# Fold in passes, one load on ScalarE's queue, x loads between the weights, a halved first q group, and three pieces of work at other places

## The chip, the cores and the metric

The kernel runs on one core of a Trainium2 chip. The metric is the device time of one execution in microseconds (us), the median of the runs. A core has five engines that run their own instruction lists side by side and wait for each other by semaphores: TensorE (PE, matmuls and transposes, results into the PSUM banks), VectorE (DVE), ScalarE (ACT), GpSimd (POOL) and SyncE (SP), which issues the loads and stores (DMAs).

## The reference

One Perceiver block in fp32 with T = 512 query rows of D = 512 and a context of 8192 rows:

```python
qp, kp, vp = LN(x) @ Wq.T + bq, ctx @ Wk.T + bk, ctx @ Wv.T + bv
x = x + softmax(qp @ kp.T / sqrt(32)) @ vp @ Wo.T + bo      # one head of width 512
q, k, v = split(LN(x) @ W_qkv); q, k = relu(rms(q)*qn), relu(rms(k)*kn)   # 16 heads of 32
x = x + (q @ (k.T @ v) / (q . sum(k) + 1e-6)) @ W_out + b_out             # linear attention
x = x + routed_experts(LN(x)) + causal_depthwise_conv(LN(x), 4 taps) + conv_b
```

The routed part has 4 gated MLPs of width 256 and 4 simple terms, and takes the best 2 of 8 for each row.

## The kernel before, in words

**Precision.** Each fp32 product is made of three fast matmuls: a matrix is split into a high part `_h` (rounded, type fp32r) and a low part `_l` (the rest), and `project` (L1400 on) sums high x high, high x low and low x high in PSUM. The high part is a copy by ScalarE (`high_...`) or GpSimd, the low part a subtraction by VectorE (`low_...`) or GpSimd (`split_wo`, `wq_l`).

**Opening.** PE multiplies `wv` by `wo` (512x512 each) in C = 4 blocks e over the contraction into four PSUM banks (`fold_part`, the fold). Block 0 has its own code (`first_part` for the first two column blocks, with 256-column halves of `wo`). A block is 12 full-width matmuls: for each c the three products one after the other. Meanwhile x (4 tiles t of 128 rows) is normalised: VectorE's `first_stats(t)`, ScalarE's `std_of(t)`, VectorE's `ln_scale(t)` (reciprocal and shift), ScalarE's `apply_of(t)`, which writes `xn`. PE transposes a tile (`transpose_x(t)`, 4 small instructions) at four places in blocks 2 and 3 of the fold; ScalarE (`high_xT`) and VectorE (`low_xT`) split it from PSUM into `xT`. Then come the q groups: for each e, 12 full-width matmuls of `wq` with all of `xT`. Each engine does its part in a hand-written order, and waits where an operand isn't there.

The loads of this stage are issued by SP one after the other: the halves of `wv` and `wo` block 0 (128 KB each), then `wv`, `wo` and x tiles (256 KB each), then `wq`, `wk` and the first context tiles.

**Attention.** The context comes in 64 tiles of 128 keys, two to a load. PE's `scores(s)` makes tile s (12 matmuls) in one of two banks, so tile s waits until VectorE's `peak(s - 2)` has taken the maximum from that bank (semaphore `max_done`), and every second tile for `low_ct`. ScalarE's `keep(s)` copies the scores to a ring first. The weighting of values follows 22 tiles later. VectorE's list in one step s is: subtractions and sums of older tiles, `low_ct` (s even), block maxima, `peak(s)`, and then odd jobs: at s = 1 `sum_key_terms()` (sums of `qb` over the four groups), at s = 3 `key_terms()` (a transpose and sums down to `key_bias`, first used at s = 17), at s = 9 `biases()`.

**Linear attention.** `linear(t)` multiplies tile t of q by the k-v product (8 PE instructions), VectorE divides by the normaliser into `heads[t]`, PE transposes (`transpose_heads(t)`), ScalarE and VectorE split, and PE projects with `wout` (12 matmuls a tile). PE's order was linear 0, 1, 2, 3, then heads 0, heads 1, then the projections.

Of the kernel before, what the change touches and what calls it, by code (L numbers as in the profile page):

```python
# [11 lines left out]
P = 128  # L12
D = 512
# [58 lines left out]
def perceiver_block(nc, x, ctx_t, ctx_n, wq_t, wk_in, wv_in, wo_t, wqkv_in, wout_in, pieces, cols_in, rows_in, out):  # L72
    with ExitStack() as stack:
# [318 lines left out]
        def _(sp):  # L392
            def load_wv(e):
                sp.dma_start(wv_raw[:, e, :], wv_in[e]).then_inc(wv_loaded[e], 16)
# [8 lines left out]
            def load_wo0(h):  # L403
                part = slice(h * HALF, (h + 1) * HALF)
                sp.dma_start(wo_raw[:, 0, part], wo_t[0][:, part]).then_inc(wo0_loaded[h], 16)

            def load_x(t):
                sp.dma_start(xs[:, t, :], x[t]).then_inc(x_loaded[t], 16)

            load_wv0(0)  # L410
            load_wo0(0)
# [5 lines left out]
            load_x(1)  # L417
            load_wo(2)
            load_wv(2)
            load_x(2)  # L420
            load_x(3)
            load_wo(3)
            load_wv(3)
            for e in range(C):
                sp.dma_start(wq_raw[:, e, :], wq_t[e]).then_inc(wq_loaded[e], 16)
# [210 lines left out]
        def _(act):  # L636
            def std_of(n):

                t = n % TT
                act.wait_ge(var_ready, n + 1)  # L640
                act.activation(std[:, t:t + 1], var[:, t:t + 1], ACT.Sqrt).then_inc(std_ready, 1)
# [23 lines left out]

            act.wait_ge(ones_ready, 1)
# [23 lines left out]
            apply_of(1)  # L690
            std_of(2)
            high_wv(3)
            high_xT(0, XT_BANKS)
            std_of(3)
            apply_of(2)
            apply_of(3)
            high_xT(1, XT_BANKS)
            high_xT(2, XT_BANKS)
            high_xT(3, XT_BANKS)
            high_wq(1)  # L700
# [184 lines left out]
        def _(dve):  # L885
# [58 lines left out]
            first_stats(0)  # L944
            first_stats(1)
            ln_scale(0)
            low_wv(2)
            ln_scale(1)
            first_stats(2)
            first_stats(3)  # L950
            low_wv(3)
            ln_scale(2)
            ln_scale(3)
            low_xT(0, XT_BANKS)
# [172 lines left out]
            for s in range(TILES + AHEAD - LEAD + 1):  # L1127
# [22 lines left out]
                if s == 1:  # L1150
                    sum_key_terms()
                if s == 3:
                    key_terms()
# [237 lines left out]
        def _(pe):  # L1391
# [34 lines left out]
            def fold_part(e, c):  # L1426

                ins = project(WVO_BANKS[c], [cut(wv, e, c * P, (c + 1) * P)], [cut(wo, e, 0, D)], starts=(e == 0),
                              stops=(e == C - 1))
                if e == C - 1:  # L1430
                    ins.then_inc(wvo_psum, 1)

# [19 lines left out]
            for c in range(2, C):  # L1452
                fold_part(0, c)

            transposed_at = {(2, 1): 0, (2, 3): 1, (3, 1): 2, (3, 3): 3}
            for e in range(1, C):
                pe.wait_ge(wv_ready, e)
                if e == 1:
                    pe.wait_ge(wo1_ready, 1)
                else:  # L1460
                    pe.wait_ge(wo_ready, e - 1)
                for c in range(C):
                    fold_part(e, c)
                    if (e, c) in transposed_at:
                        if transposed_at[e, c] == 0:
                            pe.wait_ge(ident_ready, 2)
                        transpose_x(transposed_at[e, c])

            pe.wait_ge(xl_ready, TT)
            for e in range(C):  # L1470
                pe.wait_ge(wq_ready, e + 1)
                project(Q_BANKS[e], [cut(wq, e, c * P, (c + 1) * P) for c in range(C)],
                        [cut(xT, c, 0, T) for c in range(C)]).then_inc(q_psum, 1)
# [175 lines left out]
            for t in range(TT):  # L1649
                linear(t)  # L1650
# [10 lines left out]
            transpose_heads(0)  # L1661
            transpose_heads(1)
# [153 lines left out]
```

## Time and profile before

| | |
|---|---|
| median of 3 runs | 537.34 us (537.27 to 537.45) |
| profiled execution | 536.98 us, span of its instructions 535.2 us |
| TensorE busy | 527.2 us, 99% of the span |
| VectorE, ScalarE, GpSimd busy | 363.5 (68%), 243.8 (46%), 199.2 us (37%) |
| DMA | 51.58 MB, mean 96 GB/s |
| granted TensorE clock | 1.00 of full speed |

Times inside the trace count from the span's start. In a timeline row stand start, duration, engine, line, operation, result<-operands and their count; the bracket says how long the engine had been idle and who released it. The modelled duration of a matmul runs on beside its successor's, so the pace is read from start to start. In the chain of waits each piece is what held the end back at that time.

### The profile page before, as it was taken

To read this page: it belongs to the slowest core of one execution; us is meant where nothing else is said; L and a number is where in the kernel's file an instruction comes from. 1 tells how busy PE (TensorE), PEld (TensorE's weight loads), DVE (VectorE), ACT (ScalarE), POOL (GpSimd) and SP (SyncE) were. 2 spreads that over 40 slices of the span, in tenths; PEclk is the share of its full clock that TensorE was granted. 3 is DMA by queue.
4 is the path that set the end of the run, shared out by engine and by line. 5 is a ranking of instruction groups with operands and counts; after the bars stand their busy time and mean duration, and the time that the engine had idled before them with its cause. 6 is when DMAs were issued, how large, how long until landed. Compare 5 with 4: busy or idle time off the path is not lost.

```text
span 535.2 us, 6750 instructions
## 1 busy us (share of the span) xinstructions
PE 527.2 (99%) x2434; PEld 438.2 (82%) x2434; DVE 363.5 (68%) x624; ACT 243.8 (46%) x392; POOL 199.2 (37%) x134
## 2 busy tenths in 40 slices
PE   9899999999999999999999999999999999999997
PEld 7788788888888888888888888888888888888886
DVE  5475656876567866566878554999966357538747
ACT  5652343754544544454545454557465322552210
POOL 3628041321311222234144432447449939800000
PEclk9999999999999999999999999999999999999999
DMA  8711323242332233422322221243320404200002
GB/s 295 316 37 41 119 79 118 81 157 80 106 129 80 78 87 148 155 85 80 133 104 79 80 65 55 78 159 118 137 100 21 137 1 144 93 1 0 2 0 78
DMA packets 15152, 51.58 MB, mean 96 GB/s; under 512 B 1808, under 2 KB 2320, under 8 KB 14480
## 3 DMA queue, kind: packets, MB, share of 16 engines
q1 hardware_dynamic: 15120, 51.16, 26.8%
q8 instruction: 19, 0.31, 0.2%
q14 instruction: 13, 0.11, 0.1%
HBM read 50.11 MB, written 1.05 MB: 96 GB/s over the span
## 4 chain that ended last, share of the span: by engine, by line
PE 95%; DVE 2%; DMA 1%; ACT 0%; issue 0%; SPq 0%
PE bank L1405 28%; PE bank L1513 11%; PE bank L1511 11%; PE bank L1512 11%; PE bank L1500 11%; PE bank L1502 11%; PE bank L1501 10%; PE bank L1395 1%; DMA wv_raw<-wv_in 1%; PE bank L1645 1%; PE bank L1635 1%; DVE ct_l L962 0%; PE bank L1763 0%; DVE wv_l L923 0%; DVE xT_l L913 0%
## 5 line engine op out<-in xcount | busy, mean ns | idle before, releaser
L559 POOL TENSOR_TENSOR cn_l<-raw_n,cn_h 128x1024 fp32r<-128x1024 f32 x32 | 77.7, 2427 | 197.3 <-ACT cn_h L719 197.3
L737 ACT COPY ring<-bank 128x512 f32<-128x512 f32 x64 | 37.6, 588 | 149.7 <-PE bank L1502 149.5
L1500 PE MATMUL bank<-qk_h,ct_h 128*128 128x512 f32 x256 | 99.7, 389 | 1.1 <-DVE top L1032 1.1
L1032 DVE TENSOR_TENSOR top<-top,bank 128x512 f32<-128x512 f32 x60 | 41.1, 685 | 87.4 <-ACT ring L737 86.9
L1502 PE MATMUL bank<-qk_h,ct_l 128*128 128x512 f32 x256 | 99.6, 389 | 0.0
L1501 PE MATMUL bank<-qk_l,ct_h 128*128 128x512 f32 x256 | 99.6, 389 | 0.0
L1511 PE MATMUL bank<-ph,cn_h 128*128 128x512 f32 x256 | 99.6, 389 | 0.0
L1512 PE MATMUL bank<-pl,cn_h 128*128 128x512 f32 x256 | 99.6, 389 | 0.0
L1513 PE MATMUL bank<-ph,cn_l 128*128 128x512 f32 x256 | 99.6, 389 | 0.0
L1500 PEld LDWEIGHTS bank<-qk_h,ct_h 128*128 128x128 f32 x256 | 48.0, 188 | 11.3 <-DVE ct_l L962 1.5
L1502 PEld LDWEIGHTS bank<-qk_h,ct_l 128*128 128x128 f32 x256 | 48.1, 188 | 10.1
L1512 PEld LDWEIGHTS bank<-pl,cn_h 128*128 128x128 f32 x256 | 48.1, 188 | 10.1
L1501 PEld LDWEIGHTS bank<-qk_l,ct_h 128*128 128x128 f32 x256 | 48.0, 188 | 10.0
L1511 PEld LDWEIGHTS bank<-ph,cn_h 128*128 128x128 f32 x256 | 48.1, 188 | 9.9
L1513 PEld LDWEIGHTS bank<-ph,cn_l 128*128 128x128 f32 x256 | 48.0, 188 | 9.9
L1078 DVE TENSOR_TENSOR ring<-ring,shift_b 128x512 f32<-128x512 f32 x64 | 56.0, 881 | 0.0
L744 ACT ACTIVATE ph<-ring 128x512 fp32r<-128x512 f32 x64 | 40.5, 633 | 17.7 <-PE bank L1513 9.2
L1087 DVE TENSOR_TENSOR pl<-bank,ph 128x512 fp32r<-128x512 f32 x64 | 43.7, 683 | 1.5 <-ACT bank L749 1.3
L962 DVE TENSOR_TENSOR ct_l<-raw_t,ct_h 128x1024 fp32r<-128x1024 f32 x32 | 40.8, 1278 | 2.8 <-ACT ct_h L710 2.8
L1101 DVE TENSOR_TENSOR psum_keys<-psum_keys,bank 128x512 f32<-128x512 f32 x63 | 42.6, 677 | 0.1
L749 ACT ACTIVATE bank<-ring 128x512 f32<-128x512 f32 x64 | 37.8, 591 | 1.3 <-DVE psum_keys L1101 1.3
L710 ACT CAST ct_h<-raw_t 128x1024 fp32r<-128x1024 f32 x32 | 33.4, 1044 | 0.0
(243 smaller groups left out, 862.2 us busy)
## 6 DMA issues: line engine op xcount, KB each, us to landing
raw_t<-ctx_t SPq DMA_DIRECT2D x32, 512.0 KB, 4.2
raw_n<-ctx_n SPq DMA_DIRECT2D x32, 512.0 KB, 3.3
piece_raw<-pieces SPq DMA_DIRECT2D x12, 512.0 KB, 3.3
xs<-x SPq DMA_DIRECT2D x4, 256.0 KB, 4.6
wq_raw<-wq_t SPq DMA_DIRECT2D x4, 256.0 KB, 6.0
wk_raw<-wk_in SPq DMA_DIRECT2D x1, 1024.0 KB, 7.8
w_k_raw<-wqkv_in SPq DMA_DIRECT2D x1, 1024.0 KB, 7.1
w_out_raw<-wout_in SPq DMA_DIRECT2D x1, 1024.0 KB, 5.4
```

What stands on the lines that cost most here:

```text
L559: pool.tensor_tensor(cn[p % CNB][1][:], raw_n[p % 2][:], cn[p % CNB][0][:].bitcast(F32), ALU.subtract).then_inc(cnl_ready, 1)
L1032: dve.tensor_tensor(top[:], top[:], bank[:, S_BANKS[i % 2], :], ALU.max).then_inc(max_done, 1)
L1078: dve.tensor_tensor(ring[:, q % RING, :], ring[:, q % RING, :], shift_b[q // SB % 2][:], ALU.subtract).then_inc(sub_done, 1)
L1087: dve.tensor_tensor(pl[q % PB][:], bank[:, p_bank(q), :], ph[q % PB][:].bitcast(F32), ALU.subtract).then_inc(pl_ready, 1)
L1101: dve.tensor_tensor(psum_keys[:], psum_keys[:], bank[:, p_bank(q), :], ALU.add).then_inc(den_done, 1)
L1405: ins = pe.matmul(bank[rows, dst, cols], a, b, start=(starts and c == 0 and k == 0), stop=(stops and c == n - 1 and k == 2))
L1500: pe.matmul(bank[:, dst, :], ct[i // 2 % 2][0][:, c, keys], qk[0][:, c, :], start=(c == 0), stop=False)
L1501: pe.matmul(bank[:, dst, :], ct[i // 2 % 2][0][:, c, keys], qk[1][:, c, :], start=False, stop=False)
L1502: ins = pe.matmul(bank[:, dst, :], ct[i // 2 % 2][1][:, c, keys], qk[0][:, c, :], start=False, stop=(c == C - 1))
L1511: pe.matmul(bank[:, c, :], keys[0][:, q % 2, d], ph[q % PB][:], start=first, stop=False)
L1512: pe.matmul(bank[:, c, :], keys[0][:, q % 2, d], pl[q % PB][:], start=False, stop=False)
L1513: return pe.matmul(bank[:, c, :], keys[1][:, q % 2, d], ph[q % PB][:], start=False, stop=final)
```

## The change

1. SP no longer issues the load of `wo` block 0's first half; ScalarE issues it as its first instruction. SP's x loads stand at other places among the weights.
2. The fold's blocks 1 to 3 go pass by pass: all four column blocks high x high, then all high x low, then all low x high, with PE's waits in front of the pass that reads the part. Transposes of x stand after passes, tile 3's inside the last pass. The transposed tiles 1 and 2 have new places too.
3. q group 0 is made in two column halves; the first waits only for x tiles 0 and 1.
4. ScalarE's and VectorE's lists in the opening are reordered to go with this.
5. `sum_key_terms()` moves from step 1 to step 5, `key_terms()` from 3 to 7.
6. PE's `linear(3)` moves behind `transpose_heads(0)`.

```diff
--- before.py
+++ after.py
@@ -408,19 +408,18 @@
                 sp.dma_start(xs[:, t, :], x[t]).then_inc(x_loaded[t], 16)
 
             load_wv0(0)
-            load_wo0(0)
             load_wo0(1)
             load_wv0(1)
             load_wv(1)
             load_wo(1)
             load_x(0)
-            load_x(1)
             load_wo(2)
             load_wv(2)
+            load_x(1)
             load_x(2)
-            load_x(3)
             load_wo(3)
             load_wv(3)
+            load_x(3)
             for e in range(C):
                 sp.dma_start(wq_raw[:, e, :], wq_t[e]).then_inc(wq_loaded[e], 16)
             sp.dma_start(cols[:], cols_in).then_inc(cols_loaded, 16)
@@ -663,6 +662,7 @@
                 act.wait_ge(wv_loaded[e], 16)
                 act.copy(wv[0][:, e, :], wv_raw[:, e, :]).then_inc(wv_high, 1)
 
+            act.dma_start(wo_raw[:, 0, 0:HALF], wo_t[0][:, 0:HALF]).then_inc(wo0_loaded[0], 16)
             act.wait_ge(ones_ready, 1)
             act.activation(root_table[:], ones[:], ACT.Sqrt)
 
@@ -688,16 +688,16 @@
             apply_of(0)
             std_of(1)
             apply_of(1)
+            high_wv(3)
             std_of(2)
-            high_wv(3)
             high_xT(0, XT_BANKS)
+            apply_of(2)
+            high_xT(1, XT_BANKS)
             std_of(3)
-            apply_of(2)
             apply_of(3)
-            high_xT(1, XT_BANKS)
             high_xT(2, XT_BANKS)
+            high_wq(1)
             high_xT(3, XT_BANKS)
-            high_wq(1)
             high_wq(2)
             high_wq(3)
             act.wait_ge(wk_loaded, 16)
@@ -942,16 +942,16 @@
             dve.wait_ge(wo1_high, 1)
             dve.tensor_tensor(wo[1][:, 1, :], wo_raw[:, 1, :], wo[0][:, 1, :].bitcast(F32), ALU.subtract).then_inc(wo1_ready, 1)
             first_stats(0)
+            ln_scale(0)
             first_stats(1)
-            ln_scale(0)
             low_wv(2)
             ln_scale(1)
             first_stats(2)
+            ln_scale(2)
+            low_xT(0, XT_BANKS)
             first_stats(3)
             low_wv(3)
-            ln_scale(2)
             ln_scale(3)
-            low_xT(0, XT_BANKS)
             low_xT(1, XT_BANKS)
             low_xT(2, XT_BANKS)
             low_xT(3, XT_BANKS)
@@ -1147,9 +1147,9 @@
                     shrink(s // SB - 1)
                 if s < TILES:
                     peak(s)
-                if s == 1:
+                if s == 5:
                     sum_key_terms()
-                if s == 3:
+                if s == 7:
                     key_terms()
                 if s == 9:
                     biases()
@@ -1423,13 +1423,6 @@
                 pe.wait_ge(xn_ready, t + 1)
                 transpose_tile(xn, t, XT_BANKS[t]).then_inc(xnT_psum, 1)
 
-            def fold_part(e, c):
-
-                ins = project(WVO_BANKS[c], [cut(wv, e, c * P, (c + 1) * P)], [cut(wo, e, 0, D)], starts=(e == 0),
-                              stops=(e == C - 1))
-                if e == C - 1:
-                    ins.then_inc(wvo_psum, 1)
-
             def first_part(c, h, k):
 
                 a = wv[(0, 1, 0)[k]][:, 0, c * P:(c + 1) * P]
@@ -1450,27 +1443,54 @@
                         first_part(c, h, k)
             pe.wait_ge(wv0_ready, 2)
             for c in range(2, C):
-                fold_part(0, c)
-
-            transposed_at = {(2, 1): 0, (2, 3): 1, (3, 1): 2, (3, 3): 3}
+                project(WVO_BANKS[c], [cut(wv, 0, c * P, (c + 1) * P)], [cut(wo, 0, 0, D)], stops=False)
+
+            def fold_pass(e, k):
+
+                for c in range(C):
+                    a = wv[(0, 0, 1)[k]][:, e, c * P:(c + 1) * P]
+                    ins = pe.matmul(bank[:, WVO_BANKS[c], :], a, wo[(0, 1, 0)[k]][:, e, :], start=False,
+                                    stop=(e == C - 1 and k == 2))
+                    if e == C - 1 and k == 2:
+                        ins.then_inc(wvo_psum, 1)
+                    if (e, k, c) == (C - 1, 2, 1):
+                        transpose_x(3)
+
+            transposed_at = {(2, 1): 0, (2, 2): 1, (3, 1): 2}
             for e in range(1, C):
-                pe.wait_ge(wv_ready, e)
+                pe.wait_ge(wv_high, e)
+                if e == 1:
+                    pe.wait_ge(wo1_high, 1)
+                else:
+                    pe.wait_ge(wo_high, e - 1)
+                fold_pass(e, 0)
                 if e == 1:
                     pe.wait_ge(wo1_ready, 1)
                 else:
                     pe.wait_ge(wo_ready, e - 1)
-                for c in range(C):
-                    fold_part(e, c)
-                    if (e, c) in transposed_at:
-                        if transposed_at[e, c] == 0:
-                            pe.wait_ge(ident_ready, 2)
-                        transpose_x(transposed_at[e, c])
-
-            pe.wait_ge(xl_ready, TT)
-            for e in range(C):
+                fold_pass(e, 1)
+                if (e, 1) in transposed_at:
+                    if transposed_at[e, 1] == 0:
+                        pe.wait_ge(ident_ready, 2)
+                    transpose_x(transposed_at[e, 1])
+                pe.wait_ge(wv_ready, e)
+                fold_pass(e, 2)
+                if (e, 2) in transposed_at:
+                    transpose_x(transposed_at[e, 2])
+
+            def queries_first(e, part=slice(0, T)):
+
+                pe.wait_ge(xl_ready, part.stop // P)
                 pe.wait_ge(wq_ready, e + 1)
-                project(Q_BANKS[e], [cut(wq, e, c * P, (c + 1) * P) for c in range(C)],
-                        [cut(xT, c, 0, T) for c in range(C)]).then_inc(q_psum, 1)
+                ins = project(Q_BANKS[e], [cut(wq, e, c * P, (c + 1) * P) for c in range(C)],
+                              [cut(xT, c, part.start, part.stop) for c in range(C)], cols=part)
+                if part.stop == T:
+                    ins.then_inc(q_psum, 1)
+
+            queries_first(0, slice(0, HALF))
+            queries_first(0, slice(HALF, T))
+            for e in range(1, C):
+                queries_first(e)
 
             pe.wait_ge(wk_ready, 1)
             for c in range(C):
@@ -1646,7 +1666,7 @@
                                     qrT[:, c, t * P:(t + 1) * P], kv[:, c, :], start=True, stop=True)
                 ins.then_inc(la_psum, 1)
 
-            for t in range(TT):
+            for t in range(TT - 1):
                 linear(t)
 
             def transpose_heads(t):
@@ -1659,6 +1679,7 @@
                 transpose_tile(xn, t, X2_BANKS[t]).then_inc(xnT_psum, 1)
 
             transpose_heads(0)
+            linear(TT - 1)
             transpose_heads(1)
             pe.wait_ge(w2_ready, 2 * len(W2_ORDER))
             for t in range(TT):
```

## Rows read from the trace of the kernel before

**Rows 1.** The page, busy time, share of the span and instructions of each engine.
```profile
PE 527.2 (99%) x2434; PEld 438.2 (82%) x2434; DVE 363.5 (68%) x624; ACT 243.8 (46%) x392; POOL 199.2 (37%) x134
```

**Rows 2.** PE's list of waits over the span: us in total, times, longest.
```profile
PE bank L1405 <- DVE xT_l L913: 2.5, 2, 1.4
PE bank L1500 <- DVE top L1032: 1.1, 1, 1.1
```

**Rows 3.** PE's timeline, then the chain of waits, at x's last tile.
```profile
18.64 0.60 PE L1395 MATMUL bank<-ident,xn 128*128 128x128 f32 x4
...
18.81 0.45 PE bank L1395 x4
19.28 0.59 ACT xT_h L647
...
20.65 22.05 PE bank L1405 x96
```

**Rows 4.** PE's timeline between blocks 0 and 1 of the fold.
```profile
7.97 0.39 PE L1405 MATMUL bank<-wo_h,wv_l 128*128 128x512 f32 x1
8.50 0.47 PE L1405 MATMUL bank<-wo_h,wv_h 128*128 128x512 f32 x1
```

**Rows 5.** The chain in the FFN's half-width matmuls.
```profile
465.85 7.41 PE bank L1405 x60
```

**Rows 6.** Timelines of SP, ScalarE; DMA issues: KB each, us to landing.
```profile
1.17 0.89 SPq L405 DMA_DIRECT2D wo_raw<-wo_t  x2
...
0.73 1.28 ACT L667 ACT_TABLE_LOAD   x1 [0.73 <-PEq L1809]
3.07 0.40 ACT L672 CAST wv_h<-wv_raw 128x256 fp32r<-128x256 f32 x1 [0.84 <-DMA wv_raw<-wv_in]
...
wq_raw<-wq_t SPq DMA_DIRECT2D x4, 256.0 KB, 6.0
...
wo_raw<-wo_t SPq DMA_DIRECT2D x2, 128.0 KB, 2.2
```

**Rows 7.** VectorE's and ScalarE's timelines, normalisation of x.
```profile
13.00 0.69 DVE L897 BATCH_NORM_STATS2 stats<-xs 128x6 f32<-128x512 f32 x1
...
14.01 0.83 DVE L923 TENSOR_TENSOR wv_l<-wv_raw,wv_h 128x512 fp32r<-128x512 f32 x1
...
12.11 0.81 ACT L654 ACTIVATE xn<-xs,shift,rstd 128x512 f32<-128x512 f32 x1 [0.48 <-DVE shift L906]
```

**Rows 8.** PE's and VectorE's timelines at score tiles 3 to 8.
```profile
53.18 0.39 PE L1502 MATMUL bank<-qk_h,ct_l 128*128 128x512 f32 x1
54.63 0.47 PE L1500 MATMUL bank<-qk_h,ct_h 128*128 128x512 f32 x1 [1.06 <-DVE top L1032]
...
66.10 0.39 PE L1500 MATMUL bank<-qk_h,ct_h 128*128 128x512 f32 x1
...
49.39 1.25 DVE L990 TENSOR_TENSOR qb<-qb 128x1024 f32<-128x1024 f32 x1
...
51.58 2.31 DVE L962 TENSOR_TENSOR ct_l<-raw_t,ct_h 128x1024 fp32r<-128x1024 f32 x1
...
55.61 0.70 DVE L1003 STREAM_TRANSPOSE flipped<-qb 128x512 f32<-128x512 f32 x1
...
57.84 1.20 DVE L962 TENSOR_TENSOR ct_l<-raw_t,ct_h 128x1024 fp32r<-128x1024 f32 x1
...
66.45 0.69 DVE L1032 TENSOR_TENSOR top<-top,bank 128x512 f32<-128x512 f32 x1 [2.03 <-ACT ring L737]
```

**Rows 9.** PE's and VectorE's timelines at the linear attention and its heads.
```profile
441.57 3.84 PE L1645 MATMUL bank<-kv,qrT 128*128 128x132 f32 x32
...
443.30 0.76 DVE L1251 TENSOR_TENSOR heads<-bank,late 128x256 f32<-128x256 f32 x2
...
445.24 1.04 PE L1395 MATMUL bank<-ident,heads 128*128 128x128 f32 x8
...
447.33 0.47 PE L1405 MATMUL bank<-w_out_h,xT_h 128*128 128x512 f32 x1 [1.05 <-DVE xT_l L913]
```

## The prediction

> **What bounds the kernel now.** I read the page's busy times first: TensorE (PE) is busy for 99% of the span, and no other engine for more than 68% [rows 1]. So a change gains only where it removes PE work or PE idle time. The diff removes no PE work: the same matmuls come in another order, twelve of them cut in two. I therefore read PE's list of waits [rows 2]. Beyond the wait at the very start it holds 2.5 us in two waits for `xT_l`, 1.1 us in one wait for `top`, and a short one for `wv_l`. Then the chain of waits and the timeline gave the place of each. One `xT_l` wait is at 20.65 us, where the first q group waits for the last transposed tile of x [rows 3]; the `wv_l` wait is at the border between two blocks of the fold. The `top` wait is at 54.63 us, before the fifth score tile [rows 8]. The second `xT_l` wait is at 447.33 us, before the output projection [rows 9]. PE's timeline shows one more hole that the list doesn't name: 7.97 to 8.50 us, where a slot of 0.23 would have ended at 8.20 [rows 4]. The diff touches each of these places and no other, so the sum has three terms.
>
> **Term A, the opening (fold, x, first q group).** Steady slots first: 96 full-width (512-column) matmuls in 22.05 us are 0.23 each; four transposes cost 0.45 [rows 3]. The fold up to 8.20 us is untouched. Then:
>
> PE side. Pass 0 of each block needs high parts alone; low parts are wanted four and eight slots (0.9 and 1.8 us) later. In block 1 PE waited for `wo_l` until 8.50; now it goes on at 8.20. Block 1 ends at 8.20 + 12 x 0.23 = 10.96. Block 2's first two passes end at 12.80, where the transposes of tile 0 stand; 0.45 for them and four matmuls later, at 14.17, stand tile 1's; block 3 begins at 14.62 and tile 2's stand at 16.46. Tile 3's stand inside pass 2, 0.45 + 2 x 0.23 later, at 17.37.
>
> VectorE and ScalarE side. From the start of tile 3's transposes (18.64 in the timeline, which the chain counts from 18.81) to PE's release at 20.65 were 2.0 us, with 0.59 of it on ScalarE [rows 3]. So `xT_l` of tile 0 ends at about 12.80 + 1.95 = 14.75. Behind it on VectorE stand `first_stats(3)` (1.01 from its start at 13.00 to the next instruction at 14.01), `low_wv(3)` (0.83 in the trace beside GpSimd [rows 7]; 0.6 by half of the 1.20 for twice the width [rows 8], which I take as GpSimd is idle then) and `ln_scale(3)` (0.4, an estimate from the two small instructions behind the statistics, which took 1.01 - 0.69 = 0.32). The shift is there at 14.75 + 2.0 = 16.75 and `apply_of(3)`, 0.81 [rows 7], ends at 17.55. PE wants it at 17.37: 0.2 of stall is left, tile 3 goes at 17.6 and the fold ends at 17.6 + 0.45 + 0.46 = 18.5. The first half of q group 0 needs only tiles 0 and 1, converted by then. Half-width matmuls take 7.41 / 60 = 0.1235 [rows 5], so a half is 1.48 and the cut costs 2 x 1.48 - 12 x 0.23 = 0.2: the first half ends at 20.0. The second needs `xT_l` of tile 3: on ScalarE `high_xT(2)`, `high_wq(1)` and `high_xT(3)` stand behind `apply_of(3)`, 0.55 to 0.59 each, so 19.2, and 0.7 on VectorE makes 19.9. It is just hidden. Group 1 begins at 20.0 + 1.48 = 21.5. Before, it began at 20.65 + 12 x 0.23 = 23.4. Gain 1.9.
>
> What stands behind the moved steps: `high_wq(1)`, done near 18.7, now precedes `high_xT(3)`. GpSimd's `wq_l` for group 1 follows it; even at the 2.31 of a subtraction twice as wide beside another engine [rows 8] it is ready at 21.0, 0.5 before use. `high_wv(3)` precedes `std_of(2)`, which has over a microsecond. On the SP queue x1, x2 and x3 keep their order but go behind more weights: `load_wo(2)` and `load_wv(2)` now precede x1, and `load_wo(3)` and `load_wv(3)` precede x3, so x1 and x3 land two transfers later and the weights sooner. x3 now stands just ahead of the `wq` loads; with their 6.0 us to landing [rows 6] and an issue near 6.4 it is there at 12.4, and is read at 14.7.
>
> The load given to ScalarE. SP's two issues of `wo0` halves took 0.89 [rows 6], so all later SP loads are issued about 0.45 sooner. ScalarE pays one issue (0.45, by SP's) before its table load; its first cast waited for data until 3.07, so this costs nothing. `wo0(0)` is wanted right after, near 3.4; issued at about 0.75 and landing 2.2 later [rows 6], it is there at 3.0. The first cast still waits for `wv0(0)`, so PE starts no sooner.
>
> Bounds. If all PE idle in this stretch went, group 1 would begin at 8.20 + 36 x 0.23 + 4 x 0.45 + 24 x 0.1235 = 21.25, a gain of 2.15. Downward: a subtraction on VectorE stretches when GpSimd works beside it (2.31 against 1.20 [rows 8], so up to 0.55 at half the width). If `low_wv(2)` does so and the loads land no sooner, tile 1's shift, `high_wv(3)` on ScalarE and with it `xT_h(0)` slide by 0.55, and the chain to tile 3 with them: gain 1.35. I take 1.9, since loads issued 0.45 sooner absorb most of the slide.
>
> The Trainium skill (DMA: Bandwidth & Descriptors, "Issuing engines are not separate DMA queues") says that loads issued by different engines share the same 16 DMA engines, so only issue time is saved. No row says how much of the opening is bound by issue. If the rule is read strictly, and the engines were full, the landings stay as they were and term A sits between 1.35 and 1.9; by the rows of SP's issue it is 1.9.
>
> **Term B, the key-term sums.** Tile 4's scores need the maximum of tile 2. VectorE's order was: peak(1), the two qb sums (49.39 to 51.58, so 2.2), `low_ct(2)` (51.58, 2.31), peak(2) [rows 8]. PE would have gone on at 53.18 + 0.23 = 53.41; it started at 54.63. With the sums gone, `low_ct(2)` starts at 49.39 or when ScalarE's cast of it is there (I reckon 49.8); even at 2.31 it ends at 52.1, and peak(2), 0.7, at 52.8: 0.6 to spare. Gain 54.63 - 53.41 = 1.22, and the slower slots behind a stall: 54.63 to 66.10 holds 50 slots, 11.47 against 50 x 0.227 = 11.35, so 0.1 more: 1.3.
>
> What is late next: the sums now follow peak(5), which started two tile times (12 x 0.227 = 2.72) before peak(7)'s 66.45, at 61.0, and ends at 61.7. With the sums (2.2 at most), `low_ct(4)` (1.2) and peak(6) (0.7) VectorE is done at 65.8; PE needs it for tile 8 at 66.10 [rows 8]. `key_terms` (2.2, 55.61 to 57.84) follows peak(7), done at 67.1; then 1.2 and 0.7 give 71.2 against 71.57 for tile 10 (24 slots after 66.10). Both are hidden, by 0.3 and 0.4; all these times are those of the trace before and shift together. Were a cover gone, only the excess would cost. `key_bias` is first used 10 tiles later. Bounds: 0, if the wait only moves, and 1.35; I take 1.3.
>
> **Term C, heads' transposes.** The 32 instructions of `linear` take 3.74 to 3.84 us [rows 9], 0.93 per tile. The heads of tile 0 are ready at 443.30 + 0.76 = 444.06, but PE did `linear(3)` first and transposed at 445.24; the projection started 2.09 later, at 447.33. Now the transposes start after three tiles, 441.57 + 2.81 = 444.4, and the projection at 446.5. PE's own work in between (linear(3) 0.93, 8 transposes 0.9) ends at 446.3, so it fits. Gain 0.8. VectorE behind it: heads 2 start when `xT_l` of tile 0 is done, as before, so they move along. linear(3) ends 0.5 later than before; VectorE wants it only after two more tiles of heads and two of `xT_l`. Bounds 0.6 and 0.95 (2.09 can't shrink below the stall of 1.05).
>
> **Sum.** 1.9 + 1.3 + 0.8 = 4.0. Between and behind the three places PE shows no wait [rows 2], so the gains reach the end. The profiled execution took 536.98 (span 535.20 and 1.78 around it): 533.0 for it, and 533.3 against the median of 537.34, which is 0.36 above the profiled execution.
>
> **Rivals.**
> 1. The opening is held by VectorE or ScalarE: tile 3's xn or `xT_l` later than reckoned, as eight small steps are in series. For: my margins there are 0 to 0.5 us. Against: each step's length has a row. Term A falls to 0.3 to 1.2: total 2.4 to 3.3, time 534 to 535.
> 2. The sums' wait only moves: sums or `key_terms` make tile 8 or 10 late. For: margins of 0.3 and 0.4. Against: the 2.2 for the sums was itself taken beside busy GpSimd, idle there now. It would have to eat 1.3: time 534.6.
> 3. ScalarE's load is late because the 1.28 us table load goes first: issue at 2.0 (0.73 + 1.28 [rows 6]), landing 4.2, cast 0.8 late, and everything down to the fold's end 0.8 late: 534.1.
> 4. Slower: the same load in its own queue lands much later than 2.2 us. It stands at the head of ScalarE's and PE's order, wanted 2.65 after its issue (3.4 - 0.75), so each microsecond over 2.65 is paid in full. Break-even at 2.65 + 4.0 = 6.7 us, slower by 1.07 at 7.7: 538.4 there. For: nobody used that queue before. Against: 128 KB loads took 2.1 to 2.3 us, at the emptiest moment.
> 5. No effect on the time, because a later wait takes it all back: 537.3. Against: PE has no other wait, so nothing behind runs on a clock of its own but the DMA loads.
>
> **Chances.** Forecast (532.9 to 533.9) 0.60; rival 1 0.18; rival 2 0.07; rival 3 0.06; rival 4 0.03; rival 5 0.03; 0.03 for unnamed. The range goes from all three upper bounds (4.4, and 0.2 for the uncertainty of the median) up through rivals 1 to 3: 532.7 to 535.1. A measurement here can tell 0.2%, 1.07 us, from no change. Faster by more: all but rivals 4 and 5 and part of the rest, 0.92; within: 0.05; slower: 0.03.
>
> **What would show it.** Right: no hole at 8.20; q group 1 at 21.3 to 22.1; PE's list without `top`; the last `xT_l` wait at 0.1 to 0.3 us instead of 1.05. Wrong: a wait of PE for `xn` over 0.5 us in block 3; the first fold matmul later than in the trace before; a new wait for `top` at tile 8 or 10; matmuls that change bank each time and then take more than 0.23, which no row here excludes (0.05 each would cost 1.8).

## The result, and the profile after

The changed kernel took 532.75 us (median of 4 runs, 532.70 to 534.55) against 537.31 for the kernel before, measured beside it: a ratio of 0.9921, 95% interval 0.9905 to 0.9936, or 4.6 us less. Forecast were 533.3 and a range of 532.7 to 535.1. One of the four runs, the one of 534.55, shows a granted clock of 0.997 where the others show 1.0; the median and the interval contain it, and it is left out of what follows. The profiled execution took 532.71 with a span of 530.6, before 536.98 with 535.20: 4.6 us of span went, and the time around it is 0.3 larger.

First the page of the kernel after: engines, then the queue that ScalarE's load made new.

```profile
PE 526.2 (99%) x2446; PEld 438.7 (83%) x2446; DVE 362.4 (68%) x624; ACT 243.7 (46%) x392; POOL 198.9 (37%) x134
...
q10 hardware_dynamic: 144, 0.13, 0.1%
```

PE is as full as before [rows 1], with twelve more matmuls; q10 is the one load in ScalarE's queue. PE's list of waits after:

```profile
PE bank L1416 <- POOL ones L466: 0.9, 1, 0.9
PE bank L1405 <- DVE xT_l L913: 0.2, 1, 0.2
```

The start's 0.9 is as before. The wait for `top` and the long one for `xT_l` [rows 2] are gone; the 0.2 that is left stands before the output projection. PE's timeline of the kernel after, at the opening, at score tiles 8 and 10 and at the heads:

```profile
4.14 0.76 PE L1430 MATMUL bank<-wo_h,wv_h 128*128 128x256 f32 x2
...
7.83 0.39 PE L1405 MATMUL bank<-wo_h,wv_l 128*128 128x512 f32 x1
8.05 1.07 PE L1452 MATMUL bank<-wo_h,wv_h 128*128 128x512 f32 x4
...
12.59 0.60 PE L1395 MATMUL bank<-ident,xn 128*128 128x128 f32 x4
...
16.22 0.60 PE L1395 MATMUL bank<-ident,xn 128*128 128x128 f32 x4
16.57 0.71 PE L1452 MATMUL bank<-wo_h,wv_l 128*128 128x512 f32 x2
17.37 0.66 PE L1395 MATMUL bank<-ident,xn 128*128 128x128 f32 x4
17.78 0.70 PE L1452 MATMUL bank<-wo_h,wv_l 128*128 128x512 f32 x2
18.32 0.28 PE L1405 MATMUL bank<-xT_h,wq_h 128*128 128x256 f32 x1
...
21.19 0.40 PE L1405 MATMUL bank<-xT_h,wq_h 128*128 128x512 f32 x1
...
62.48 0.39 PE L1520 MATMUL bank<-qk_h,ct_h 128*128 128x512 f32 x1
...
67.95 0.39 PE L1520 MATMUL bank<-qk_h,ct_h 128*128 128x512 f32 x1
...
437.95 2.94 PE L1665 MATMUL bank<-kv,qrT 128*128 128x132 f32 x24
440.73 0.60 PE L1395 MATMUL bank<-ident,heads 128*128 128x128 f32 x4
441.16 1.07 PE L1665 MATMUL bank<-kv,qrT 128*128 128x132 f32 x8
442.07 0.60 PE L1395 MATMUL bank<-ident,heads 128*128 128x128 f32 x4
442.82 0.47 PE L1405 MATMUL bank<-w_out_h,xT_h 128*128 128x512 f32 x1 [0.15 <-DVE xT_l L913]
```

Block 1 of the fold starts at 8.05, 0.22 after the matmul before it: the hole of [rows 4] is gone. Twenty slots and no transposes lie between 8.05 and 12.59, so a slot is 0.227 although each matmul goes to another PSUM bank than the last. Tile 3's transposes come at 17.37. Tile 2's began at 16.22; with 0.45 for them (the first matmul behind transposes takes 0.1 more than a slot, which is in the 0.45) and two slots, tile 3's could have come at 17.12, so 0.25 of hole is left there, which the list of waits doesn't name. The 24 half-width matmuls from 18.32 run without a gap at 0.12 each, and group 1 starts at 21.19.

VectorE's timeline after, at x's last tile and at the score tiles:

```profile
13.85 0.69 DVE L913 TENSOR_TENSOR xT_l<-bank,xT_h 128x512 fp32r<-128x512 f32 x1
14.45 0.69 DVE L897 BATCH_NORM_STATS2 stats<-xs 128x6 f32<-128x512 f32 x1
...
15.46 0.68 DVE L923 TENSOR_TENSOR wv_l<-wv_raw,wv_h 128x512 fp32r<-128x512 f32 x1
...
18.83 0.69 DVE L913 TENSOR_TENSOR xT_l<-bank,xT_h 128x512 fp32r<-128x512 f32 x1 [0.32 <-ACT xT_h L646]
...
47.46 1.60 DVE L962 TENSOR_TENSOR ct_l<-raw_t,ct_h 128x1024 fp32r<-128x1024 f32 x1 [0.26 <-ACT ct_h L710]
...
58.00 1.22 DVE L990 TENSOR_TENSOR qb<-qb 128x1024 f32<-128x1024 f32 x1
59.25 0.69 DVE L992 TENSOR_TENSOR qb<-qb 128x512 f32<-128x512 f32 x1
59.86 1.22 DVE L962 TENSOR_TENSOR ct_l<-raw_t,ct_h 128x1024 fp32r<-128x1024 f32 x1
61.00 0.68 DVE L1032 TENSOR_TENSOR top<-top,bank 128x512 f32<-128x512 f32 x1
...
66.81 0.67 DVE L1032 TENSOR_TENSOR top<-top,bank 128x512 f32<-128x512 f32 x1
```

And ScalarE's, at the start and at tile 3, with the DMA issues of `wo` behind it (KB each, us to landing):

```profile
0.73 0.40 ACTq L665 DMA_DIRECT2D wo_raw<-wo_t  x1
1.17 1.28 ACT L667 ACT_TABLE_LOAD   x1 [1.17 <-PEq L1830]
...
3.29 0.40 ACT L672 CAST wv_h<-wv_raw 128x256 fp32r<-128x256 f32 x1 [0.62 <-DMA wv_raw<-wv_in]
...
16.50 0.81 ACT L653 ACTIVATE xn<-xs,shift,rstd 128x512 f32<-128x512 f32 x1 [0.72 <-DVE shift L906]
```

```profile
wo_raw<-wo_t ACTq DMA_DIRECT2D x1, 128.0 KB, 2.7
wo_raw<-wo_t SPq DMA_DIRECT2D x1, 128.0 KB, 2.6
```

The two profiled executions, put side by side at points that both have, give the three terms. Group 1 went from 23.49 to 21.19: 2.30 for the opening. From group 1 to the output projection it was 423.84 and is 421.63: 2.21, of which the stretch from the first linear attention matmul to the projection gives 5.76 - 4.87 = 0.89 ([rows 9] and above) and the sums the other 1.32. The sum is 4.51 of the 4.6.

### The profile page after: what moved, and what is told of

Read it like the earlier page. It is cut to its first block, busy times and chain, and to the rows that moved or that the text cites. A ratio compares the mean times of both kernels' runs of the same rounds, so it can differ in the third digit from the quotient of the medians.

```text
span 530.6 us, 6778 instructions
## 1 busy us (share of the span) xinstructions
PE 526.2 (99%) x2446; PEld 438.7 (83%) x2446; DVE 362.4 (68%) x624; ACT 243.7 (46%) x392; POOL 198.9 (37%) x134
## 2 busy tenths in 40 slices
DMA packets 15152, 51.58 MB, mean 97 GB/s; under 512 B 1808, under 2 KB 2320, under 8 KB 14480
## 4 chain that ended last, share of the span: by engine, by line
PE 95%; DVE 2%; ACT 1%; DMA 1%; SPq 0%; issue 0%
PE bank L1405 26%; PE bank L1520 11%; PE bank L1531 11%; PE bank L1533 11%; PE bank L1521 11%; PE bank L1522 11%; PE bank L1532 11%; PE bank L1395 1%; DMA wo_raw<-wo_t 1%; PE bank L1655 1%; PE bank L1665 1%; DVE stats L897 0%; ACT xn L653 0%; DVE xT_l L913 0%; PE bank L1784 0%; DVE wv_l L923 0%
```

## The experiments

e1, e2 and e12 start from the kernel before, the others from the changed one. The intervals of the ratios are 0.2 to 0.3% wide and overlap for kernels that differ by less than 1 us, so small differences are read from the spans, the median with its range, and from places in the trace. The kernel before had a median span of 535.6 (e1 to e4), 535.5 (e5 to e8) and 535.4 (e9 to e12) beside them.

| run | median us | ratio, 95% | span, median (range) |
|---|---|---|---|
| e1_key_terms | 535.77 | 0.9972 (0.9958 to 0.9985) | 534.0 (533.3 to 534.9) |
| e2_linear | 536.53 | 0.9980 (0.9971 to 0.9989) | 534.7 (533.7 to 535.0) |
| e3_opening | 535.00 | 0.9966 (0.9955 to 0.9977) | 533.1 (532.8 to 533.7) |
| e4_sp_load | 532.89 | 0.9918 (0.9904 to 0.9931) | 531.0 (530.3 to 531.4) |
| e5_after_again | 533.04 | 0.9920 (0.9908 to 0.9933) | 531.0 (530.4 to 531.3) |
| e6_whole_q | 534.02 | 0.9940 (0.9927 to 0.9952) | 532.2 (531.9 to 532.7) |
| e7_fold_by_c | 535.42 | 0.9965 (0.9953 to 0.9978) | 533.1 (532.7 to 533.3) |
| e8_stats3_first | 532.66 | 0.9917 (0.9903 to 0.9930) | 530.5 (530.4 to 530.7) |
| e9_both_at_5 | 534.78 | 0.9958 (0.9945 to 0.9970) | 532.7 (532.2 to 532.8) |
| e10_x_order | 532.99 | 0.9927 (0.9915 to 0.9940) | 531.0 (530.9 to 531.7) |
| e11_old_lists | 533.47 | 0.9930 (0.9917 to 0.9942) | 530.7 (530.5 to 531.0) |
| e12_passes_alone | 533.36 | 0.9928 (0.9914 to 0.9942) | 531.6 (531.3 to 532.9) |

**Each term alone.** e1 is the kernel before with the sums moved only, e2 the kernel before with the heads' transposes moved only, e3 the changed kernel with both undone.

```diff
-                if s == 1:
+                if s == 5:
                     sum_key_terms()
-                if s == 3:
+                if s == 7:
                     key_terms()
```

```diff
-            for t in range(TT):
+            for t in range(TT - 1):
                 linear(t)
...
             transpose_heads(0)
+            linear(TT - 1)
             transpose_heads(1)
```

> The kernel before with only the sums moved to step 5 and key_terms to step 7. My theory, that the three places add up and nothing behind them waits: PE's wait for top is gone, tile 8 starts 1.3 us earlier, time 536.0 (1.3 less, 1.1 to 1.4). Rival, that gains in this part are swallowed by a later wait: 537.3. Rival, that the wait only moves to tile 8 or 10: a new wait for top there, 536.5 to 537.3.

> The kernel before with only linear(3) moved behind the first tile's transposes. My theory: the projection starts 0.85 us earlier and PE's wait for xT_l falls from 1.05 to below 0.3; time 536.45 (0.8 to 0.95 less). Rival, that VectorE's later tiles, which get linear(3) later, hold the layer norm behind it: 0 to 0.5 less.

> The changed kernel with the key terms and linear(3) back at their old places, so the opening alone is changed. My theory: 2.3 us less, 535.0, with q group 1 starting at 21.2 instead of 23.5. Rival, that part of the 2.3 came from the pace of the first matmuls changing earlier by chance (it did by 0.15 to 0.4) and not from the edit: 1.9 less, 535.4, group 1 at 21.6.

The spans fell by 1.6, 0.9 and 2.5: together 5.0, where the kernel with all three terms (e4, beside them, which lacks only ScalarE's load) lost 4.6, well within the ranges of the table. The profiles are sharper, since they leave the opening's scatter out: from group 1 to the projection e1 takes 422.50 and e2 422.95, against 423.84. So the sums give 1.34 and the heads 0.89 alone, and 1.32 and 0.89 in company. The terms add, and none moves its wait into another place. PE's list of waits of e2 keeps the wait for `top`:

```profile
PE bank L1405 <- DVE xT_l L913: 1.6, 2, 1.4
PE bank L1500 <- DVE top L1032: 1.1, 1, 1.1
```

In e1's list the wait for `top` is missing and the two `xT_l` waits are those of before:

```profile
PE bank L1405 <- DVE xT_l L913: 2.5, 2, 1.4
```

**How near the sums come to their next wait.** e9 runs `key_terms` at step 5 too, right behind the sums.

```diff
                 if s == 5:
                     sum_key_terms()
-                if s == 7:
+                if s == 5:
                     key_terms()
```

> The changed kernel with key_terms directly behind the sums, both at step 5: the margin that step 7 leaves is spent on purpose. My theory of term B (VectorE's list in front of a tile's maximum counts in full, less its slack): behind peak(5), which ends at 58.1, stand 1.8 of sums, 2.2 of key terms, 1.2 of ct_l and 0.7 of peak(6), done at 63.95, while tile 8 wants to start at 62.5. PE waits 1.5 for top there, once: 534.3 to 534.6, against 532.9. Rival, that the moved work is cheap wherever it stands and the old wait was due to GpSimd working beside it at steps 1 to 3: 0 to 0.3 more.

PE's timeline of e9 at tile 8:

```profile
62.65 0.40 PE L1561 MATMUL bank<-bv_parts_l,ones_r 128*128 128x512 f32 x1
64.58 0.47 PE L1520 MATMUL bank<-qk_h,ct_h 128*128 128x512 f32 x1 [1.53 <-DVE top L1032]
```

The 2.24 of `key_terms` put ahead of peak(6) bring a wait of 1.53 at tile 8, so 0.7 of cover is there without it; the span is 1.7 over e10's, measured beside it. The second rival's mechanism is real, and at tile 8 the move stops 0.7 to 0.8 us short of it. Tile 10 is nearer: in the changed kernel peak(8) ends at 67.48 and tile 10 starts at 67.95, so 0.5 is left there behind `key_terms` at step 7.

**ScalarE's load and the loads' order.** e4 gives the first half of `wo0` back to the SP queue, e5 is the changed kernel once more, e10 puts SP's x loads back where they were.

```diff
             load_wv0(0)
+            load_wo0(0)
             load_wo0(1)
...
-            act.dma_start(wo_raw[:, 0, 0:HALF], wo_t[0][:, 0:HALF]).then_inc(wo0_loaded[0], 16)
```

```diff
             load_x(0)
+            load_x(1)
             load_wo(2)
             load_wv(2)
-            load_x(1)
             load_x(2)
+            load_x(3)
             load_wo(3)
             load_wv(3)
-            load_x(3)
```

> The changed kernel with the first half of wo block 0 loaded by SP again, as second load. Theory 1, that ScalarE's load brings nothing: with it the first load landed 0.2 us later and the fold began at 4.14 instead of 3.92, and what the other loads gained wasn't needed. Then the fold starts at 3.92 here, group 1 at 21.0 to 21.2, time 532.6 to 532.8. Theory 2, my prediction's: the 0.45 us of issue is what keeps VectorE's chain from sliding; then tile 1's shift is 0.3 to 0.5 later, tile 3's transposes too, time 533.0 to 533.3.

> The changed kernel itself, beside the others of this call. All theories: 532.6 to 533.0; q group 1 at 21.2, with up to 0.3 either way from the opening's own scatter (first fold matmul at 3.92 or 4.14, slow pace of the first matmuls ending between 5.5 and 7.0).

> The changed kernel with SP's x loads in the old order. My theory: every load of this stage is read later than it lands in either order (wo 2 at 8.5, wv 2 at 9.3, x1 at 9.8), but for wo 2 and wv 2, which land 0.65 later here and are wanted by PE at 10.8: no change, 532.8 to 533.1, group 1 within 0.1. Rival, my prediction's fear of a slide: the later weights push high_wv(2) and the normalisation behind it, 0.3 to 0.6 more.

All three have a median span of 531.0. The load in ScalarE's queue does what it says (issued at 0.73, ahead of the table load) and is worth nothing that the spans show; the same holds for the order of x among the weights. Group 1 starts at 21.21, 21.50 and 21.55. Why freeing the SP queue earlier brings nothing shows in the windows of the changed kernel after the first fold matmul (window, length, busy us with counts of PE, its weight loads, VectorE, ScalarE and GpSimd, then granted clock, DMA share, GB/s):

```profile
3.90:5.50 1.60, 1.60 (x8) 1.44 (x8) 1.15 (x4) 0.82 (x4) 0.00 (x0) 1.00 0.91 308
5.50:7.00 1.50, 1.50 (x10) 1.46 (x9) 0.89 (x2) 0.82 (x2) 0.00 (x0) 1.00 0.96 307
```

The 16 DMA engines are busy for 91 to 96% there (79 and 98% in the same windows of e5), so the loads wait mostly for them and little for their issue. The landings agree: SP issues x's first load at 3.06 in the changed kernel and at 3.52 in e4, but a load of x takes 5.4 us to landing against 4.7 (median of the four), so it ends no sooner. By these rows the rule of the Trainium skill (DMA: Bandwidth & Descriptors, "Issuing engines are not separate DMA queues"), that another issuing engine saves issue time alone, agrees with this trace.

The order of x does move one thing inside the opening, as GpSimd's and VectorE's timelines of e10 show:

```profile
9.95 1.30 POOL L477 TENSOR_TENSOR wo_l<-wo_raw,wo_h 128x512 fp32r<-128x512 f32 x1
```

```profile
10.66 1.13 DVE L923 TENSOR_TENSOR wv_l<-wv_raw,wv_h 128x512 fp32r<-128x512 f32 x1
```

`low_wv(2)` takes 0.97 to 1.27 in all six profiles with the old order (before, e1, e2, e10, e11, e12), where it starts beside GpSimd's `wo_l`, and 0.68 in all eight with the new one, where `wo` block 2 lands sooner and `wo_l` is done. That is the stretch that the prediction feared for term A. The spans don't show it: e10's equals e5's, and e11's is no longer.

**What of the opening carries the gain.** Four variants. e6 does q group 0 in one piece. e7 does the fold column by column as before, with the changed lists of ScalarE, VectorE and SP. e11 keeps passes and halves, with all those lists and loads as before. e12 is the kernel before with the fold by passes, the sums and the heads: no halves, and old lists.

Of e11 ScalarE's part is shown; VectorE's and SP's go back in the same way. Of e12 the diff against the changed kernel would be those of e6 and e11 together.

```diff
-            queries_first(0, slice(0, HALF))
-            queries_first(0, slice(HALF, T))
-            for e in range(1, C):
+            for e in range(C):
                 queries_first(e)
```

```diff
-                fold_pass(e, 0)
...
-                fold_pass(e, 1)
...
-                fold_pass(e, 2)
...
+                for c in range(C):
+                    fold_part(e, c)
+                    if (e, c) in transposed_at:
```

```diff
             apply_of(1)
+            std_of(2)
             high_wv(3)
-            std_of(2)
             high_xT(0, XT_BANKS)
+            std_of(3)
             apply_of(2)
+            apply_of(3)
             high_xT(1, XT_BANKS)
-            std_of(3)
-            apply_of(3)
             high_xT(2, XT_BANKS)
+            high_xT(3, XT_BANKS)
             high_wq(1)
-            high_xT(3, XT_BANKS)
```

> The changed kernel with q group 0 in one piece, so that it waits for all four x tiles. My theory: PE has its operands for half the columns at 18.3 but the last low part at 19.55, so the whole group starts at 19.65 and group 1 at 22.4: 1.2 more, 533.9, and a wait for xT_l of 1.1. Rival, that halves cost what they hide, as each half-width matmul runs at 0.12 instead of 0.115: 532.7 to 532.9.

> The changed kernel with the fold's blocks column by column again, low parts wanted at once, all lists of the other engines as changed. My theory: the new lists only fit the passes. Block 2 waits for wv_l until 11.5 (0.6), block 3 until 16.2 (1.4), less what the transposes cover: 1.5 to 2.2 more, 534.3 to 535. Rival, that the passes only closed the hole before block 1: 0.2 to 0.5 more, 533.0 to 533.3.

> The changed kernel with all loads and both reordered lists as before; what stays of the opening's change are PE's passes and the halves. My theory from the rows: the old lists have xn of tile 3 at 16.7, before PE wants it (17.0), and xT_l of tile 3 at 19.0, before the second half (19.4). So PE has no hole at tile 3 and group 1 starts at 20.9 to 21.1: 532.4 to 532.8, no slower than the changed kernel. Rival, that the lists and loads carry part of the 2.3 us: 0.3 to 1.0 more than the changed kernel, 533.3 to 534.

> As the run before, with q group 0 whole as well: of the opening only the passes are new. My theory: the fold ends at 17.9, group 0 waits for xT_l of tile 3 until 19.0 and group 1 starts at 21.8: 533.3 to 533.6. So the passes are worth 1.7 of the opening's 2.3 and the halves 0.6 to 0.9 beside the old lists. Rival, that passes bring little where the lists weren't fitted to them: 534.5 to 535.

e6: the span grows by 1.2 over e5's; PE waits 1.08 for `xT_l` of tile 3 before group 0, as the kernel before did, and group 1 starts at 23.26. From the last two matmuls of the fold to group 1 it is 4.66 against e5's 3.42, so the halves are worth 1.2 here. (The rest of the way to e5's 21.50 is a longer hole at tile 3 in e6's profile, the slowest of its five.)

e7: the span grows by 2.1 over e5's, so nearly the whole gain of the opening goes although the lists are the changed ones and group 0 is still halved. Of the 2.4 that are left of the gain, the sums and the heads make 2.23. The time is 0.4 above my range: block 3 waits until 16.98, not 16.2. Its PE timeline:

```profile
8.48 0.47 PE L1405 MATMUL bank<-wo_h,wv_h 128*128 128x512 f32 x1 [1.07 <-DVE wo_l L943]
...
16.98 0.50 PE L1405 MATMUL bank<-wo_h,wv_h 128*128 128x512 f32 x1 [1.18 <-DVE wv_l L923]
```

and its VectorE timeline:

```profile
14.62 0.69 DVE L913 TENSOR_TENSOR xT_l<-bank,xT_h 128x512 fp32r<-128x512 f32 x1 [0.58 <-ACT xT_h L646]
15.23 0.68 DVE L897 BATCH_NORM_STATS2 stats<-xs 128x6 f32<-128x512 f32 x1
...
16.24 0.68 DVE L923 TENSOR_TENSOR wv_l<-wv_raw,wv_h 128x512 fp32r<-128x512 f32 x1
```

`low_wv(3)` now stands behind `low_xT(0)` and the statistics of tile 3. Column by column the block can't start without it; by passes the first eight matmuls of the block (1.8 us) do without, and the same lateness is hidden.

e11: with the old lists and the old loads the span is 530.7, no more than that of e10 (531.0). Tile 3's transposes follow two slots behind (16.78, 17.32), a wait of 0.3 for `wv_h` stands in block 2 instead, and group 1 starts at 21.25. Its time, 533.47, is in the rival's range of 533.3 to 534, but the time around the span was 2.7 in its runs (median) and 2.0 in e10's; inside the span nothing is longer. So passes and halves are the whole gain, and beside them the reordered lists bring nothing that can be measured.

e12: the span is 3.8 below that of before, 2.23 of it the sums and the heads, so 1.6 are the passes' (and 0.9 more, to e11, the halves'). Halves without passes were not run, so what they bring alone is not shown. e12's profiled execution was the slowest of its five, 1.3 above their median. The rows are PE's timeline, then ScalarE's:

```profile
7.11 0.39 PE L1405 MATMUL bank<-wo_h,wv_l 128*128 128x512 f32 x1
9.25 1.15 PE L1452 MATMUL bank<-wo_h,wv_h 128*128 128x512 f32 x4 [1.75 <-ACT wo_h L685]
```

```profile
8.49 0.62 ACT L685 CAST wo_h<-wo_raw 128x512 fp32r<-128x512 f32 x1 [1.07 <-DMA wo_raw<-wo_t]
```

The load of `wo` block 1 landed 5.4 us after its issue there, against 3.9 in the kernel before and 4.2 in the one after. Passes don't help against that: pass 0 needs the high part. Why it landed so late stays open.

**The hole left at tile 3.** e8 puts tile 3's statistics, standard deviation and scale one place earlier each.

```diff
             apply_of(2)
+            std_of(3)
             high_xT(1, XT_BANKS)
-            std_of(3)
             apply_of(3)
...
             ln_scale(2)
+            first_stats(3)
             low_xT(0, XT_BANKS)
-            first_stats(3)
+            ln_scale(3)
             low_wv(3)
-            ln_scale(3)
```

> An attempt to go further: VectorE takes the statistics of x tile 3 ahead of xT_l of tile 0, and its shift ahead of wv_l of block 3; ScalarE takes its std ahead of xT_h of tile 1. My theory: tile 3's xn is ready near 16.6 instead of 17.3, PE's 0.35 us hole before its transposes goes, group 1 at 20.85, 0.35 less than the changed kernel: 532.4. Rival, that then wv_l of block 3 (wanted at 16.6) or xT_l of tile 3 becomes late and takes it back: within 0.1 of it.

PE's timeline of e8:

```profile
16.23 0.60 PE L1395 MATMUL bank<-ident,xn 128*128 128x128 f32 x4
16.63 0.73 PE L1452 MATMUL bank<-wo_h,wv_l 128*128 128x512 f32 x2
17.20 0.60 PE L1395 MATMUL bank<-ident,xn 128*128 128x128 f32 x4
...
20.98 0.40 PE L1405 MATMUL bank<-xT_h,wq_h 128*128 128x512 f32 x1
```

The hole is gone: the two slots from 16.63 to tile 3's transposes take 0.57, where it was 0.80 in the changed kernel, and from tile 2's transposes to group 1 it is 4.75 against 4.97. That is the hole of 0.25 within 0.03; the 0.35 that I expected counted 0.1 that belongs to the transposes themselves. It is the fastest version of all, 532.66, with a span 0.5 below that of the changed kernel beside it (530.4 to 530.7 against 530.4 to 531.3); ranges that touch and ratios that overlap don't show that it is faster. The trace shows 0.2 at that place.

## Why the prediction was right

**The frame held.** PE was the bound at 99%, the time could only come from its idle places, and all that came did: 4.51 of 4.6 at the three places named, the rest after the projection. Forecast were 4.0. By terms: A 1.9 forecast, 2.30 in the pair of profiles; B 1.3 and 1.32; C 0.8 and 0.89. The total was near its edge all the same: 532.75 lies below the band that had 0.60 (532.9 to 533.9) and 0.05 above the lower end of the range. On which side of 532.9 a median falls is chance: the same kernel gave 533.04 in e5.

**Term A was sized 0.4 too low, above its own upper bound of 2.15.** In the working's order: block 1 begins at 8.05, reckoned 8.20 (0.15), because the stretch before it, which I took as untouched, was itself shorter this time; 36 slots at 0.227 instead of 0.23 give 0.11, 24 half-width matmuls at 0.12 instead of 0.1235 give 0.09; 0.06 is my rounding up of 21.44 to 21.5, and group 1 before began at 23.49, not 23.4 (0.09). Against it stand 0.05 more for the transposes and 0.05 more of hole at tile 3, 0.25 for 0.2. The hole came nearly as reckoned because both sides were early by the same amount: `apply_of(3)` ended at 17.31, reckoned 17.55, and PE wanted it at 17.12, reckoned 17.37. The bound was too low because it took the start of block 1 as fixed and the pace rounded up. The start isn't fixed: with equal code the kernel before had group 1 at 23.49, 23.62 (e1) and 24.22 (e2), the changed one at 21.19 and 21.50. From such pairs A is 2.0 to 3.0, so the size of a pair's A holds to some tenths at best; the spans say 2.5 (e3). Of the signs that I named, two came out against me without the mechanism failing: group 1 began at 21.19, below my 21.3 to 22.1, and the first fold matmul came later than before (4.14 for 3.92), which I had called a sign of being wrong.

**Which edit of A works.** The prediction gave A as a whole. Passes give about 1.6, halves on top of them 0.9 to 1.2; the order of the lists, x's place among the loads and ScalarE's load nothing that can be measured. The sentence that loads issued 0.45 sooner absorb most of a slide was wrong: the loads don't end sooner by it. The slide stayed away for another reason, the new order of x, by which `low_wv(2)` no longer meets GpSimd's `wo_l` (0.68 in e4 too, which lacks ScalarE's load). So 1.9 instead of 1.35 was the right choice for a wrong reason. Nor does the slide cost what the lower bound says: where `low_wv(2)` stretches beside the passes (e10, e11), the span is no longer.

**Term B.** PE's stall is gone, and the cost of a slow slot behind it too (1.34 in e1, 1.3 forecast). The margins for the next waits were reckoned 0.3 and 0.4. The first is 0.8 (peak(6) ends at 61.68, tile 8 is at 62.48), since the sums took 58.00 to 59.86, 1.86, with GpSimd idle, not the 2.2 that I carried over from [rows 8]. The second is 0.5 (peak(8) and tile 10).

**Term C.** 4.87 from the first linear matmul to the projection, reckoned 4.93. The wait that I expected to shrink is 0.15.

**The rivals.** The first (the opening held by VectorE or ScalarE) was there as the hole of 0.25 at tile 3. It is 0.5 to 0.6 in the profiles of e3, e6, e9 and e10: in e3 block 1 starts at 7.93, 0.12 sooner than in the changed kernel, and group 1 at 21.43, 0.24 later. So a further gain of PE ahead of tile 3 would be taken back there in part. The second exists, with margins of 0.8 at tile 8 (e9) and 0.5 at tile 10. The third falls: the DMA stands in ScalarE's timeline at 0.73, ahead of the table load at 1.17. The fourth falls: the load landed after 2.7 us, longer than the 2.2 taken and 0.05 above the point from which I said it would be paid; yet little was paid. The wait of ScalarE's first cast, for `wv_raw` and not for `wo_raw`, ends at 3.22 to 3.33 in the eight profiles with ScalarE's load and at 2.88 to 3.07 in the six without it, so `wv`'s first half lands 0.2 to 0.4 later beside it. The first fold matmul comes at 4.08 to 4.19 with it and at 3.92 to 4.14 without, 0.1 later in the mean, and the spans of e4 and e5 are the same. The fifth falls with the result. The doubt about matmuls that change bank each time falls with 0.227 a slot.

## What to carry to other kernels

Where each operand is split in a high and a low part and the low one is made later, run all products of the high parts first across the columns (each in its own PSUM bank) instead of finishing column by column: it gives one late part four and the other eight slots of slack in a block of twelve, and a slot costs no more for it here (0.227). Reorder helper engines' lists with such slack in view: with these lists and without the passes only about 0.2 of the opening's 2.3 to 2.5 us was left (e7), and the old lists did as well beside the passes (e11). When a stall comes from work that isn't due, move that work behind the wait and count the next deadline in the same table: here margins of 0.8 and 0.5 us held, and 2.2 us more work broke the first by 1.5.

## What was not expected of the hardware

- The opening scatters with equal code: the first fold matmul starts at 3.92, 4.12 and 4.14 in before, e1 and e2. The first 256-column matmuls come 0.21 apart, later ones 0.12. The slow pace ends near 4.2 in e12 and near 6.5 in the changed kernel, while the granted clock is recorded as 1.00 (the 2.4 GHz level) in all those windows. What ends it stays open. Where it ends early, PE only waits for `wo_h` (0.5 in e8 and e9, 1.8 in e12), so part of it is lost.
- One load of 256 KB, `wo` block 1, landed after 3.9, 4.2 and 5.4 us in three profiles.
- VectorE's subtraction that makes `ct_l` (128 x 1024) took 2.31 in the kernel before, 1.60 and 1.22 in the changed one. GpSimd works beside it in the longer ones, as the prediction assumed. GpSimd's rows, of the kernel before and of the changed one, give the size:

```profile
51.19 1.61 POOL L518 TENSOR_TENSOR bv_parts_l<-bv_wo,bv_parts_h 128x512 fp32r<-128x512 f32 x1
```

```profile
47.37 0.61 POOL L515 CAST bv_parts_h<-bv_wo 128x512 fp32r<-128x512 f32 x1
```

The first ends at 52.80, 1.22 after VectorE's start at 51.58, and VectorE ends 1.09 after that. The second ends at 47.98, 0.52 after VectorE's start at 47.46, and VectorE ends 1.08 after that. So in both the subtraction takes what GpSimd's running instruction still had to go and then about the time that it takes alone. `low_wv(2)` in e10 fits: 0.59 to the end of `wo_l` at 11.25, then 0.54 of a subtraction that takes 0.68 alone.
